# Two-precision convolution: the low kind's clip on GpSimd, and bands of 8, 6, 6 and 8 row pairs

## The reference, cut to what matters

```
def _quant_act_uint(x, scale, bits):
    n = 2.0 ** bits - 1.0
    return jnp.clip(_round_ste(x / scale), 0.0, n) * scale
...
mask = _predictor_mask(x)
x_high = jnp.where(mask, x, EPS)
x_low = jnp.where(mask, EPS, x)
y_high = _conv(_quant_act_uint(x_high, act_scale_high, 8), _quant_weight_per_oc(w_high, 8))
y_low = _conv(_quant_act_uint(x_low, act_scale_low, 4), _quant_weight_per_oc(w_low, 4))
return y_high + y_low
```

## Time and profile before

| | |
|---|---|
| median of 3 runs | 638.43 us (637.63 to 640.11) |
| profiled execution, its own time | 637.6 us |
| its span | 635.8 us |
| busy share of PE, DVE, ACT, POOL | 96%, 91%, 78%, 13% |
| moved by DMA | 152.25 MB, 239 GB/s |

### The profile page before, as it was taken

How to read it: one execution, slowest core, us unless ns; L and a number is a source line. 1 busy time by engine, 2 the same in 40 slices (tenths; PEclk the granted TensorE clock), 3 DMA queues, 4 the chain that set the end, 5 groups by cost and what they waited for, 6 DMA issues and landing times.

```text
span 635.8 us, 10658 instructions
## 1 busy us (share of the span) xinstructions
PE 608.5 (96%) x3528; PEld 340.9 (54%) x3528; DVE 577.4 (91%) x739; ACT 496.2 (78%) x522; POOL 83.7 (13%) x90
## 2 busy tenths in 40 slices
PE   2779999999999999999999999999999999999996
PEld 1344555555555555555555555555555555555553
DVE  7959999999999999999999999999999999999944
ACT  5669678888877888887787888778788777888543
POOL 3311111101011110110111010111111011100000
PEclk9889999999999999999999999999999999999999
DMA  7488888788988888899788879888788988873222
GB/s 276 152 257 231 257 260 240 255 271 256 303 255 251 245 237 258 273 300 292 218 225 247 264 270 303 246 265 249 205 270 280 302 239 255 237 228 117 87 102 102
DMA packets 48010, 152.25 MB, mean 239 GB/s; under 512 B 2688, under 2 KB 30048, under 8 KB 44032
## 3 DMA queue, kind: packets, MB, share of 16 engines
q1 hardware_dynamic: 14400, 103.95, 40.8%
q0 software_dynamic: 33600, 48.17, 37.6%
HBM read 100.73 MB, written 51.38 MB: 239 GB/s over the span
## 4 chain that ended last, share of the span: by engine, by line
PE 92%; DVE 3%; ACT 2%; issue 1%; DMA 1%; DVEq 0%; SPq 0%; ACTq 0%
PE psum L363 91%; DVE ybuf L742 1%; ACT rounded_h L474 1%; DMA wraw_l<-w_low 1%; ACT psum L509 1%; ACT wT_h L491 0%; DVE planes L677 0%; ACT wT_l L491 0%; DVE inner L698 0%; DVE outer L713 0%; DVE pooled L648 0%; DVE w_max_l L602 0%; DVE middle L735 0%; ACT shared L530 0%; DVE rowsums L689 0%
## 5 line engine op out<-in xcount | busy, mean ns | idle before, releaser
L509 ACT ACTIVATE psum<-psum,ratio 128x448 f32<-128x448 f32 (+2 forms) x190 | 186.9, 987 | 104.7 <-PE psum L363 103.7
L363 PE MATMUL psum<-planes,wT_l 128*128 128x448 f16 (+1 forms) x792 | 166.2, 360 | 0.3 <-DVE ybuf L742 0.3
L363 PE MATMUL psum<-planes,wT_h 128*128 128x448 f16 (+1 forms) x792 | 163.8, 356 | 0.0
L363 PEld LDWEIGHTS psum<-planes,wT_l 128*128 128x128 f16 x792 | 78.2, 99 | 77.8 <-issue 2.8
L363 PEld LDWEIGHTS psum<-planes,wT_h 128*128 128x128 f16 x792 | 76.7, 97 | 76.8 <-issue 1.5
L474 ACT ACTIVATE rounded_l<-xbuf,inv_act_l 128x1568 int16<-128x1568 f32 (+1 forms) x64 | 101.7, 1591 | 4.8 <-DMA xbuf<-x 4.8
L474 ACT ACTIVATE rounded_h<-xbuf,inv_act_h 128x1568 int16<-128x1568 f32 (+1 forms) x64 | 101.9, 1594 | 0.0
L530 ACT ACTIVATE shared<-psum,bias,out_scale_h 128x448 f32<-128x448 f32 (+1 forms) x128 | 86.3, 674 | 14.6 <-PE psum L363 13.5
L742 DVE SCALAR_TENSOR_TENSOR ybuf<-psum,out_scale_h,shared 128x448 f32<-128x448 f32 x132 | 85.3, 676 | 7.6 <-ACT shared L530 5.9
L329 POOL DMA_DIRECT2D halves<-x x30 | 44.8, 1492 | 346.8 <-DMA halves<-x 346.8
L363 PE MATMUL psum<-rowsums,wT_l 128*128 128x448 f16 (+1 forms) x384 | 87.1, 336 | 2.3 <-ACT wT_l L491 2.3
(11 more groups left out here) (75 smaller groups left out, 478.3 us busy)
## 6 DMA issues: line engine op xcount, KB each, us to landing
xbuf<-x SPq DMA_DIRECT2D x31, 1568.0 KB, 9.0
halves<-x POOLq DMA_DIRECT2D x60, 784.0 KB, 11.2
y<-ybuf SPq DMA_DIRECT2D x32, 896.0 KB, 7.1
y<-ybuf SPq DMA_DIRECT2D x32, 672.0 KB, 7.3
xbuf<-x SPq DMA_DIRECT2D x1, 896.0 KB, 7.9
xbuf<-x SPq DMA_DIRECT2D x1, 672.0 KB, 5.2
wraw_l<-w_low SPq DMA_DIRECT2D x1, 576.0 KB, 4.1
wraw_h<-w_high SPq DMA_DIRECT2D x1, 576.0 KB, 6.2
```

The source lines that it names most:

```text
L363: last = nc.tensor.matmul(out, wT[k][:, mat, :], moving(k, p, band, row, dx), start=(k == "l" and j == 0), stop=(j == len(parts) - 1), ski ...
L509: return nc.scalar.activation(banks, banks, ACT.Identity, scale=ratio[:, 0:1])
```

## The change

It has four parts. The bands become 8, 6, 6 and 8 pairs; bands 2 and 3 stay the four-product ones, so these now cover 14 pairs instead of 12, and `inner` and `outer` grow with them. The store is cut at 14 pairs instead of 16. From image 2 on GpSimd clips the low kind, in two parts of 1568 elements, after `outer` of the image before is formed; a small addition into `gate` stands ahead of it. GpSimd's order is now: first DMA of image m+1, clip of image m, adding DMA of image m+1. DVE keeps the high clip, and waits ahead of the low mask for GpSimd's two parts; ACT waits for them before it overwrites `rounded` of the low kind. `rounded` and `halves` become one tensor each for both buffers.

```
-    BAND = ((0, 8), (8, 8), (16, 4), (20, 8))
+    BAND = ((0, 8), (8, 6), (14, 6), (20, 8))
...
-        halves = [sb(f"halves{p}", [P, BY, POOL // 2 * W], F32) for p in range(2)]
+        halves = sb("halves", [P, 2, BY, POOL // 2 * W], F32)
...
+            def begin_halves(m, p):
+                pool.wait_ge(s_pooled, prepared(m - 2))
+                nc.gpsimd.dma_start(halves[:, bass.ds(p, 1), :, :], image_halves(m)[:, :, 0, :]).then_inc(s_half, 16)
+            def add_halves(m, p):
+                pool.wait_ge(s_half, 16 * (m - 1))
+                nc.gpsimd.dma_start(halves[:, bass.ds(p, 1), :, :], image_halves(m)[:, :, 1, :], accum_op=ALU.add
+                                    ).then_inc(s_halves, 16)
+            def clip_low(m, p):
+                pool.wait_ge(s_round["l"], 2 * m + 2)
+                pool.wait_ge(s_plane["l"], prepared(m - 1))
+                pool.wait_ge(s_outer, m - 1)
+                nc.gpsimd.tensor_tensor(gate[:, :], one[:, :], one[:, :], ALU.add)
+                for part in (slice(0, HW // 2), slice(HW // 2, HW)):
+                    nc.gpsimd.tensor_scalar(clipped["l"][:, part], rounded["l"][p][:, part],
+                                            2.0 ** BITS["l"][0] - 1.0, q_eps["l"][:, 0:1], ALU.min, ALU.subtract
+                                            ).then_inc(s_late_clip, 1)
+            begin_halves(2, 0)
+            add_halves(2, 0)
+            with pool.Fori(1, B // 2 - 1) as i:
+                for p in range(2):
+                    m = 2 * i + p
+                    begin_halves(m + 1, 1 - p)
+                    clip_low(m, p)
+                    add_halves(m + 1, 1 - p)
...
@@ apply_mask
-                dve.wait_ge(s_clip[k], prepared(n, 1 if q is None else q))
+                if k == "l" and not early(n):
+                    dve.wait_ge(s_late_clip, 2 * (n - 1))
+                else:
+                    dve.wait_ge(s_clip[k], prepared(n, 1 if q is None else q))
...
@@ body of DVE, step n
                 if ahead > 0:
-                    clip("l", m, mp)
                     clip("h", m, mp)
```

## The result

The changed kernel is slower by a fifth: 763.62 us (median of 4 runs, 762.96 to 764.73) against 639.27 for the kernel before beside it (637.63 to 640.14), a ratio of 1.1964 (1.1919 to 1.2009). The profiled execution took 763.96 us, its span is 762.1. The forecast was 633.5.

What follows compares the result with a forecast made beforehand. PE was taken as the bound, full from image 2 on, with DVE second. Terms -8.6 + 3.8 + 0.3 = -4.5 us gave 633.5 us, own range 631.5 to 635.5, wider range 631 to 652.

Steps and rivals of the forecast that it cites:

- PE's work: PE's products under the new bands: 18.29 us an image, 0.288 us less, -8.6 us over images 2 to 31.
- DVE's image and the deadlines: DVE's image falls from 17.60 to 17.26 us, staying second to PE; output rows meet PE's needs with 0.8 us or more.
- the wait ahead of `middle`: DVE's wait for ACT's `shared` in band 2: still 0.5 us, a sign that DVE has room.
- The clip on GpSimd: Low clip on GpSimd after `outer`: two parts of 1.7 us, 3.55 us with `gate`, hidden within 7.6 us.
- the term of 3.3 us: Length of GpSimd's two clip parts together, extrapolated from its tensor-scalars at 2 and 122 elements.
- My upper bound, 6.9 us: Longest clip considered, scaled from instructions beside a busy DVE; with `gate` 7.15 of 7.6 us, just hidden.
- The window of 7.6 us: Time in each image from the end of `outer` until GpSimd's clip is needed, after the next high clip.
- the rivals: Clip about 6.6 us: 637, 0.16; cheap start: 631, 0.08; `chosen` shut out: 656, 0.17; late landing: 638 to 645, 0.07.
- The lock: DVE and GpSimd shut each other out for whole instructions; only `chosen` may be caught, losing 0.2 us, hidden, between parts.
- The halves' DMAs and the end: Adding DMA behind the clip lands in 11 to 13 us, cost 0; larger last store, +0.3 us.
- The start: At image 2, the first clipped by GpSimd, low mask at 61.5 and PE at about 75.2 instead of 71.43: +3.8 us.

Runs made afterwards that it cites:

- bands_only: The kernel before with only the bands changed to 8, 6, 6 and 8; VectorE keeps the low clip: 632.32 us against 637.3, ratio 0.9914.
- no_min: The changed kernel with GpSimd's two clip parts using add and multiply, the low kind's upper clip left out from image 2: 635.66 us against 639.34, ratio 0.995.
- forms: The kernel before with a row of GpSimd instructions of various forms appended behind the last output row, other engines idle: 711.11 us.
- half_four_parts: The changed kernel with GpSimd clipping the first half of the low kind in four parts of 392, DVE the rest: 639.39 us against 639.34, ratio 1.0017.
- half_clip: The changed kernel with GpSimd clipping only the first 1568 elements of the low kind, DVE the rest ahead of its high clip: 720.91 us, ratio 1.1283.
- half_after_choose: The same split as `half_clip`, with GpSimd's part started only after `chosen`: 675.16 us, ratio 1.0579.
- after_choose: The changed kernel with GpSimd's clip held back until DVE has also formed `chosen` of the same image: 819.57 us, ratio 1.2847.
- eight_parts: The changed kernel with the clip cut into eight GpSimd instructions of 392 elements instead of two parts: 829.98 us, ratio 1.2994.
- early_two: The changed kernel without GpSimd's wait for `outer`, so the clip may start earlier: 787.03 us, ratio 1.2322.
- forms_two: The kernel before with more GpSimd forms, including single operations and other pairs, run alone behind its end: 732.2 us.

## Why the prediction was wrong, step by step

- **PE's work: right.** 0.288 us less an image were forecast; `bands_only` has 18.625 - 18.339 = 0.286, `no_min` 0.283. That 8.6 us are not seen in full in the time of `bands_only` is the start's doing.
- **DVE's image and the deadlines: right where the clip is short.** In `no_min` PE waits for nobody from image 2 on, and the wait ahead of `middle`, forecast as 0.5 us, is 0.61.
- **The clip on GpSimd: the step that failed.** "GpSimd's tensor-scalars of the same two-operation form" were not of the same form. Those of rows 7 add and multiply; the clip takes a minimum and subtracts. In `forms` the first kind takes 1.57 us for 1568 elements (1.7 forecast), and the second 5.56, so the term of 3.3 us measured 11.2. Only the number of operations was matched, not which they are. My upper bound, 6.9 us, was "just hidden", and 7.0 us of clip in `half_four_parts` do hide; the true 11.2 us lie 4.3 above it. The Trainium skill ("GPSIMD Engine Reference", Performance versus the Vector engine), which I had cited for one input at 1.03 cycles an element, agrees with the quick pair and not with the others here: 5.56 and 1.57 us differ by a factor of 3.5 at one input each, so the measurement decides.
- **No case for a clip beyond its window.** The window of 7.6 us was right: in `no_min` 7.8 pass from `outer`'s end, 404.37, to the low mask, 412.18. What the prediction did not work out is the price of each us beyond it. That is the ring: as `outer` lets the clip go and the clip lets the masks go, it costs its full length in every image. The masks come 12.4 us after `outer`, and 10.1 follow: 22.5 an image, and 112 us over the run. With the ring written down, a clip of 3.4 times the forecast's length would have stood in the rivals at its price. As it was, no rival and no part of the range held the outcome.
- **The lock: the mechanism was right, its part was not the one forecast.** At the forecast's length `chosen` gets in between the two parts with 0.24 us (`no_min`), as the forecast had it. With parts of 5.56 us it is shut out to the end of the part. In `half_clip` 4.4 us pass from its start to the output rows behind the two `middle` (416.35 to 420.75), where 1.15 pass in `half_after_choose` (411.07 to 412.22), so DVE loses 3.25. In the changed kernel this and the high clip, held until the second part ends, fill DVE's 22.5 us almost wholly, yet the ring decides: the lock adds to it only the 0.75 us from the clip's end, 318.05, to the low mask, 318.80. `after_choose` and `eight_parts` take most of the lock off DVE and are slower, by the lengths that they add to the ring. In `after_choose` these are 1.9 us of `pooled` and `chosen`, 0.6 by which the clip grows, and -0.6 at the low mask, together the 1.9 measured; in `eight_parts` they are 2.6 of clip and -0.6, with 2.2 measured.
- **How far the lock goes.** The Trainium skill ("SBUF — State Buffer", Who interferes with whom) states the lock for whole instructions. The trace agrees for `chosen`, and `pooled` (1.78 us) and rows from PSUM (0.68 at 448 elements) keep their length beside the clip. It does not agree throughout. In `early_two` the held `rowsums` ends 0.52 us before the part beside it in all 15 images from 200 to 560 us, in the sample at 403.28 and 403.81; and in `eight_parts` the high clip runs within a part. There the measured rows decide, though the spans of GpSimd are rough.
- **The halves' DMAs and the end: right.** In `no_min` the adding DMA took 7.6 to 15.0 us to land, median 12.0, with 11 to 13 forecast; with the clip of 11.2 us it was 7.8 to 14.7, median 8.0. In both, only `pooled` of image 2, at the start, waits for them (9.4 and 9.0 us, once). With +0.3 at the end the account of `bands_only` closes, and that of the changed kernel to 0.6 us.
- **The start: mis-sized.** Forecast +3.8 us; +7.6 in `no_min`, where the clip has the forecast's length. Two things were missed. DVE is 2.0 us late before the clip begins, so that the low mask starts at 63.47, not 61.5: `pooled` of image 2 starts at 46.90 instead of 44.49, and the executions of the kernel before in `forms` and `forms_two` are late there as well (47.52 and 46.30). The forecast took one execution's start for the kernel's, so this part is chance as far as the runs show. And a wait of PE is paid twice: after 4.60 us of it the granted clock was 0.50 for 4.8 us, 2.4 us more. In the changed kernel it is +14.8. The range lost nothing by it: the clip decided.

Two things were not tried: whether `chosen` goes free when `pooled` lies in PSUM, and what decides when the first halves land.

## What to carry to other kernels

Price an instruction on another engine by rows of the same operations on it, not of the same count of operands; where the trace has none, say that the price is unknown and leave the range wide, or measure the instruction alone. When a helper engine is released by the end of a chain and its result releases the next turn of it, write the ring's length down: within the window the helper is free, past it each microsecond costs a microsecond in every turn. A waits view that names the helper once can hide this, since a DVE instruction that is shut out counts as busy. Before a difference of the start is laid to a change, look at the start of another execution of the same kernel.

## What the hardware showed that was not expected

- On GpSimd, 1568 elements of int16 to float16: a cast 1.49 us, add and multiply in either order 1.57, one operation alone 4.16 to 4.24, two others together 5.47 to 5.57; the two-input addition in float16 3.14.
- DVE's tensor-scalars (49 elements of `chosen`, 3136 of the high clip) beside a GpSimd part of 5.56 us are held up to its end, within 0.2 us; `chosen` gets in between two parts (0.19 to 0.38 us with parts of 392 elements or quick ones). `rowsums` and `outer`, with both inputs in SBUF, are held up as well (up to 4.07 instead of 0.99, 4.87 instead of 1.84), but not to the end: they finish 0.52 us before and 0.32 us after the part, which with their own lengths puts their release at 1.5 us before its end in both. `pooled` and the rows from PSUM are not held up.
- It can go the other way: beside DVE's high clip a part of 392 elements took 1.96 us instead of 1.60.
- A DMA's issue on GpSimd can stretch too: 2.23 us beside DVE's high clip in `half_after_choose`, 1.56 in `half_clip`, with the high clip at 1.50 instead of 1.03.
